# Two buffers of the front of a Mamba and mixture-of-experts kernel are laid elsewhere: u over x, delta over the normalised rows

## The reference

```python
xn = _layernorm(x, axis=-1)
s = ssm(xn)                      # Mamba: scan over time
g = _silu(moe(xn))               # 8 experts, top 2, capacity 1024 rows each
x = x + s * g
```

```python
xc = causal_conv(xn, conv_w) + conv_b          # 4 taps, per channel
x_conv = silu(xc)
proj = x_conv @ xproj_w.T                      # dt_in (128), B_in (16), C_in (16)
delta = softplus(dt_in @ dtproj_w.T + dtproj_b)
a = exp(delta[..., None] * A)                  # A = -exp(A_log), 16 states
b = delta[..., None] * B_in[:, :, None, :] * x_conv[..., None]
```

## Time and profile before

| | us |
|---|---|
| median of 3 runs | 2011.69 (2011.02 to 2016.66) |
| the profiled execution | 2014.59 |
| its span, first to last instruction | 2012.7 |
| work of the front ends | about 247.6 |
| the main loop begins | 254.0 |

### The profile page before, as it was taken

How to read it: one execution, slowest core, us unless ns; L and a number is a source line. 1 busy time by engine, 2 the same in 40 slices (tenths; PEclk the granted TensorE clock), 3 DMA queues, 4 the chain that set the end, 5 groups by cost and what they waited for, 6 DMA issues and landing times. The chain is left out here.

```text
span 2012.7 us, 29247 instructions
## 1 busy us (share of the span) xinstructions
PE 1847.6 (92%) x8968; PEld 1449.4 (72%) x8968; DVE 1853.9 (92%) x2004; ACT 1222.6 (61%) x1772; POOL 1303.5 (65%) x621
## 2 busy tenths in 40 slices
PE   6998189999999999999999999999999999999940
PEld 3332078888888878887888788888888888888830
DVE  7998579899998999899989998999899989999899
ACT  3577585556755665566556655666565755675543
POOL 1388466578667776677567866786678667866530
PEclk9999699999999999999999999999999999999975
DMA  9168643346212531244124511351145113621396
GB/s 315 68 97 114 172 173 116 115 162 153 74 64 103 138 86 61 73 146 109 63 73 142 120 68 64 124 121 63 63 150 127 63 63 111 177 74 63 108 355 242
DMA packets 83894, 240.06 MB, mean 119 GB/s; under 512 B 11713, under 2 KB 12609, under 8 KB 71505
## 3 DMA queue, kind: packets, MB, share of 16 engines
q1 hardware_dynamic: 67120, 205.07, 31.1%
q0 software_dynamic: 16416, 33.70, 9.2%
q10 hardware_dynamic: 256, 0.26, 0.1%
HBM read 170.45 MB, written 68.55 MB: 119 GB/s over the span
## 5 line engine op out<-in xcount | busy, mean ns | idle before, releaser
L1188 DVE TENSOR_TENSOR_SCAN a_sb<-a_sb,state,ub_sb 128x512 f32<-128x512 f32 x512 | 894.2, 1785 | 9.9 <-issue 6.0
L1097 POOL TENSOR_TENSOR ub_sb<-u_sb,brow_sb 128x1024 f32<-128x1024 f32 x256 | 629.5, 2459 | 401.7 <-DVE a_sb L1188 398.9
L829 PE MATMUL pm<-xTh,w1l 128*128 128x512 f32 x1024 | 423.0, 413 | 6.8 <-POOL w1l L1082 5.7
L829 PE MATMUL pm<-w2h,hl 128*128 128x512 f32 x1024 | 422.8, 413 | 0.2 <-DVE hl L1168 0.2
L831 PE MATMUL pm<-w2h,hh 128*128 128x512 f32 x1024 | 401.8, 392 | 0.0
L831 PE MATMUL pm<-xTh,w1h 128*128 128x512 f32 x1024 | 401.6, 392 | 0.0
L830 PE MATMUL pm<-w2l,hh 128*128 128x512 f32 x1024 | 398.6, 389 | 0.0
L830 PE MATMUL pm<-xTl,w1h 128*128 128x512 f32 x1024 | 398.1, 389 | 0.0
L1159 DVE SCALAR_TENSOR_TENSOR s_acc_keep<-pt,ct_keep,s_acc_keep 128x512 f32<-128x512 f32 x480 | 352.0, 734 | 19.7 <-PE pt L861 19.0
L976 ACT ACTIVATE a_sb<-delta_sb,neg_a_keep 128x512 f32<-128x512 f32 x512 | 330.2, 713 | 6.7
L861 PE MATMUL pt<-ident_keep,a_sb 128*128 128x128 f32 x2048 | 306.3, 272 | 5.7 <-DVE a_sb L1188 5.7
(11 more groups left out here) (163 smaller groups left out, 1950.8 us busy)
## 6 DMA issues: line engine op xcount, KB each, us to landing
raw_keep<-in_w SPq DMA_DIRECT2D x64, 1024.0 KB, 4.8
brow_sb<-b_chunks SPq DMA_DIRECT2D x128, 256.0 KB
moe_rows<-zeros SPq DMA_DIRECT2D x8, 1280.0 KB, 6.4
xn_rows<-xn_sb SPq DMA_DIRECT2D x8, 1024.0 KB, 9.1
delta_chunks<-ln_sb SPq DMA_DIRECT2D x8, 1024.0 KB
u_chunks<-xn_sb SPq DMA_DIRECT2D x16, 512.0 KB
delta_sb<-delta_chunks SPq DMA_DIRECT2D x8, 1024.0 KB, 8.1
u_sb<-u_chunks SPq DMA_DIRECT2D x16, 512.0 KB, 3.9
```

Of the source, the lines that this page charges most:

```text
L829: pe.matmul(out, sl, mh, start=start, stop=False)
L1097: pool.tensor_tensor(ub[:, h], u[:, 2 * h:2 * h + 2, :], brow[:, m % 2:m % 2 + 1, :].to_broadcast([P, 2, CH]), ALU.mult).then_inc(s_["bmul ...
L1188: op = dve.tensor_tensor_scan(abuf[:, m, 2 * h + k, :], abuf[:, m, 2 * h + k, :], ub[:, h, k, :], state[:, ds(col, 1)], ALU.mult, ALU.add)
```

## The change

Delta gets the two places of `xn`, and u is written over x in `xnT` and stored from there. `ln` holds the logarithm alone. With that the waits change: ACT's wait ahead of the logarithm is now for DVE's delta of the chunk before; DVE waits ahead of delta, not ahead of u, and for the delta stores of two chunks before; the two semaphores of u's stores become one and the one of delta's becomes two.

```diff
-        u_now = xn
+        d_now = xn
...
-            lnz rounded dropped soft delta u_done delta_out u_out0 u_out1 neg_a ct ct_copied first_rows first_weight
+            lnz rounded dropped soft delta u_done delta_out0 delta_out1 u_out neg_a ct ct_copied first_rows first_weight
...
             def store_du(ch):
                 sp.wait_ge(s_["delta"], 2 * ch + 2)
                 apart(sp, s_["sp_at"])
-                sp.dma_start(dr.delta[ch], ln[:]).then_inc(s_["delta_out"], 16)
+                sp.dma_start(dr.delta[ch], d_now[:, ch % 2]).then_inc(s_[f"delta_out{ch % 2}"], 16)
                 for n, h in enumerate(HALVES):
                     sp.wait_ge(s_["u_done"], 2 * ch + n + 1)
                     apart(sp, s_["sp_at"])
-                    sp.dma_start(dr.u[ch, :, h], u_now[:, ch % 2, h]).then_inc(s_[f"u_out{ch % 2}"], 16)
+                    sp.dma_start(dr.u[ch, :, h], xnT[:, ch, h, HALO:]).then_inc(s_["u_out"], 16)
...
-            sp.wait_ge(s_["delta_out"], 16 * NCH)
             for u in range(2):
-                sp.wait_ge(s_[f"u_out{u}"], 32 * NCH // 2)
+                sp.wait_ge(s_[f"delta_out{u}"], 16 * NCH // 2)
+            sp.wait_ge(s_["u_out"], 32 * NCH)
...
                 if ch > 0:
-                    act.wait_ge(s_["delta_out"], 16 * ch)
-                    act.wait_ge(s_["u_done"], 2 * ch)
+                    act.wait_ge(s_["delta"], 2 * ch)
...
+                if ch >= 2:
+                    dve.wait_ge(s_[f"delta_out{ch % 2}"], 16 * (ch // 2))
+                else:
+                    dve.wait_ge(s_[f"xn_out{ch}"], 16 * NCH // 2)
                 for n, h in enumerate(HALVES):
                     dve.wait_ge(s_["soft"], 2 * ch + n + 1)
                     dve.wait_ge(s_["lnz"], 2 * ch + n + 1)
-                    dve.tensor_tensor(ln[:, h], ln[:, h], back[:, h], ALU.add).then_inc(s_["delta"], 1)
-                if ch >= 2:
-                    dve.wait_ge(s_[f"u_out{ch % 2}"], 32 * (ch // 2))
-                else:
-                    dve.wait_ge(s_[f"xn_out{ch}"], 16 * NCH // 2)
+                    dve.tensor_tensor(d_now[:, ch % 2, h], ln[:, h], back[:, h], ALU.add).then_inc(s_["delta"], 1)
                 for n, h in enumerate(HALVES):
                     dve.wait_ge(s_["delta"], 2 * ch + n + 1)
-                    dve.tensor_tensor(u_now[:, ch % 2, h], ln[:, h], xnT[:, ch, h, HALO:], ALU.mult).then_inc(s_["u_done"], 1)
+                    x = xnT[:, ch, h, HALO:]
+                    dve.tensor_tensor(x, d_now[:, ch % 2, h], x, ALU.mult).then_inc(s_["u_done"], 1)
```

## The result

The changed kernel took 2029.11 us (median of 5 runs, 2024.73 to 2055.22) beside 2011.95 for the kernel before; the ratio is 1.0064 (95% interval 1.0049 to 1.0080). It is slower by more than the 0.3% that can be told apart, and lies 14 us above the end of the range. The same kernel profiled once more (e1, 2032.47) is nearer the median, so both are shown.

The account below looks back on a forecast made before the run. GpSimd's chain of scatters and gathers was taken to end the front. Of ACT's 17.7 us, 2.9 would be gained and the rest wait at the barrier: from the median of 2011.69 to 2008.8 us, range 1998.5 to 2015.0.

Parts of the forecast that it names:

- GpSimd's drain and the main loop stay: Behind the front's gathers: GpSimd's drain of 6032 ns and the main loop keep their length, adding nothing to the sum.
- step 2: DVE's delta in the front: its wait for the store of two chunks ago costs nothing, covered by 4 us.
- Step (5): GpSimd's scatters and gathers: last scatter issued by 213, landed at 224.5, gathers landed at 244.6 against 247.5.
- Idle DVE is free until chunk 4: DVE in the front: no idle time until chunk 4 is done, so nothing of ACT's matters before; afterwards DVE waits for ACT.
- Step (1): ACT's wait before the logarithms goes: logarithms 5 to 7 ready at 189.9, 204.3, 215.1; chunk 7 ends 17.7 us earlier.
- Steps (3) and (4): u written over x costs nothing; its store in 2 KB pieces costs some 0.15 us a chunk, hidden.
- D: Rival, u's stores: 2 KB pieces hold the scatters longer and POOL stalls once more, 2022.2 us; chance 0.08.
- C: Rival, store bursts back to back: last scatter lands at 230 to 236, 0.2 gained to 5.8 us lost; chance 0.15.
- B: Rival, scatters slip through: last lands between 216 and 218, gathers at 235.4 to 237.4, 1999.6 to 2001.6 us; chance 0.30.
- E: Rival: the wait only moves from ACT to DVE's wait for the store of two chunks back, 2007 to 2012 us; chance 0.04.
- What would show it: Signs in the front's profile: right, DVE's last u by 223 to 225; wrong, last gather before 241 or after 249.

Follow-up runs that it names:

- e1: The changed kernel with no edit, profiled again: median 2029.41 us, ratio 1.0062 to the kernel before.
- e6: The changed kernel with one more one-operand DVE operation in each chunk's soft: 2013.84 us, ratio 1.0004 to the kernel before.
- e7: The changed kernel, 8 semaphore increments added, DVE waiting ahead of soft of chunks 1 to 6 for counts of issued scatters: 2010.87 us, ratio 0.9983.
- e5: The changed kernel with 8 semaphore increments added at the end of DVE's front program: 2022.28 us, ratio 1.0048.
- e10: The changed kernel with 4 semaphore increments at the end of DVE's front program in place of 8: 2019.48 us (one run).
- e2: The kernel before with no edit, profiled again: 2013.75 us (one run).
- e3: The changed kernel with ACT's wait for the delta store and u of the chunk before put back: 2021.82 us, ratio 1.0038.
- e4: The kernel before with DVE's wait for u's place moved ahead of delta: 2022.20 us, ratio 1.0036.
- e8: The kernel before with 128 semaphore increments added at the end of DVE's front program: 2014.38 us (one run).
- e9: The changed kernel with ACT's wait put back and 8 semaphore increments on DVE, e3 and e5 together: 2014.07 us, ratio 1.0001.
- e11: The changed kernel, 8 increments added, DVE waiting ahead of soft of chunks 1 to 5 for 22, 33, 44, 55 and 64 scatters: 2006.31 us, ratio 0.9966.

## Why the prediction was wrong

**"GpSimd's drain and the main loop stay".** The drain stayed, at 6032 ns. The main loop did not: it took 7.4 us more in the profile after, 1765.0 to 1766.3 us in every profile of a kernel whose DVE program is 8 instructions shorter, and 1757.9 to 1759.0 in all the others. The change merges one wait per chunk, as the wait for a place now stands together with those for `soft` and for the logarithm; I had costed the moved wait by what it waits for (step 2, rightly nothing in the normal case) and not by its instruction. This term of the sum was missing, and by itself it was worth more than all that I gained. It enters at the jump back and right behind it: DVE idles 1.8 to 2.0 us ahead of the first scan in the four short kernels and 1.1 to 1.5 in the ten others, and from there to the sixteenth operation it takes 20.3 us for 19.4, but for one jump of e1, which took 19.4. Those scans run beside GpSimd's operations; that the later start changes how the two meet is likely and not shown. Why the edge lies between 8 and 4 instructions fewer isn't shown either; a page boundary near the head would do it.

**Step (5), the two long issues "as if a queue was full".** This reading failed. e6, e7 and the ends of the issues in the kernel after show them held by DVE: they end some 1 us after DVE's next convolution begins, or after an operation like its first one, or 0.8 us after DVE stops. The 17.12 and 11.31 us are the distances to the next convolution. The Trainium skill (SBUF — State Buffer, SBUF: two separate sides) says that DVE and GpSimd share a pair of ports, taken exclusively by whichever starts first, and that GpSimd's descriptors wait for it; the 27.40 us agree in kind. But it speaks of one instruction at a time, and DVE's single operations took 1.2 us: here the issue was held through the whole train. I had read the smaller form of it, 1.97 us for 0.96, and priced the missing idle time at two such issues (2.1 us). What it was worth differs from run to run: the last scatter was issued by 210.9 before, and then by 203.5 in e5, 212.9 in e10, 226.2 in e1 and 255.1 in the profile after; I had 213. In e1 the rest of the sum follows from this: the last scatter landed at 242.8 for 224.5, and GpSimd's drain began at 259.3 for 244.6.

**"Idle DVE is free until chunk 4"** was right for ACT, and its inverse, which I did not draw, is the point: the time that DVE idled at chunk 5 was GpSimd's gap behind the last convolution, 5.24 us ahead of the chunk and 7.34 in its midst. In the timeline of the kernel before:

```profile
205.33 2.36 DVE L608 TENSOR_TENSOR ln_sb<-ln_sb,back_sb 128x1024 f32<-128x1024 f32 x2 [7.34 <-ACT ln_sb L389]
```

The gap matters only when an issue is held as DVE comes to it, and that is chance: the six profiles with ACT's wait and no pacing (before, e2, e3, e4, e8, e9) have the same two long issues, while the four without it (after, e1, e5, e10) have four, two, one, and the two of before. In e5 and e10 no issue was held on past 186.5.

**Step (1)** held: the wait is gone, the logarithms of chunks 5 to 7 came at 186.8, 201.0 and 211.8 in e1 (190, 204 and 215 forecast), DVE's last operation ended at 220.3 (223.6). **Steps (3) and (4)** held, by e3 and e9. **Step (2)**, the store of two chunks ago at nothing, held where GpSimd was held (after, e1, e6, e7). It failed where the scatters flowed: DVE waited 17.5 us for such stores in e10, 4.2 in e5 and 1.9 in e11.

**The rivals.** D gave 2022.2 and was nearest by its number, which is luck: e9 has its 2 KB pieces and takes the time of before (1.0001). C (bursts back to back delay the last landing) is open: the landing took 16.7 us in e1 and 20.1 in e10, for 12.35, but 15.7 in e2 and 16.7 in e9 too, where ACT's wait kept the bursts apart. B did not occur: in e5 the last scatter landed at 218.7 and the gathers at 238.3, near B's times, but because the scatter went out early, and it took 15.2 us to land. E was seen in e10, and in e5 and e11 in small, but DVE ended e10's at 237, and GpSimd came last. **What would show it:** no wait of ACT, the drain of 6.0 us and the gathers 1.26 apart came as said, and the last u was earlier still. Of the signs of being wrong the main loop of another length and a last gather after 249 are in both profiles of the changed kernel, a third long issue only in the first.

## What to carry to other kernels

An idle time on one engine can be the time in which another gets through; before closing it, look for instructions on GpSimd whose length is many times their usual one, and at what DVE begins and ends with them. A moved or merged wait can be an instruction less: where a loop follows, compare its period before and after, and if it moved, restore the program's length before anything else is explained. And when a front varies by tens of us from run to run, one profile gives one of its ways; repeat it before reading a cause from it. Here five waits of DVE that let GpSimd through at fixed moments gained some 5 us in the kernel before, while the buffers alone lost.

## What the runs showed that I had not expected

- The same loop took 7 to 8 us more with DVE's program ahead of it 8 instructions shorter; 4 put back are enough, and 128 too many do nothing. Some 4 us of this are in scans that took longer just behind each jump.
- An issue of 0.96 us was held for up to 27.40 us by a train of DVE's operations, most of them with two operands, and an operation of 0.57 us for 9.24.
- It depends on 0.3 us how this falls out: an issue that began 0.11 us ahead of DVE's first operation was held for 11.3 us, one that began 0.16 us behind it took 1.37.
- A store of 1 MB took up to 38.0 us beside scatters of 8 bytes an entry, and the DMA engines showed as full at 125 GB/s.
